# Moving the attention stage's residual loads and result stores from ScalarE's DMA queue to GpSimd's

## The chip, the cores and the metric

One core of one Trainium2 chip runs the whole model. The metric is the time of one execution on the device, in microseconds. The core has five engines that work side by side, each through its own instructions in order: TensorE (PE in the profile; PEld is its loading of weights), VectorE (DVE), ScalarE (ACT), GpSimd (POOL) and SyncE (SP), which only issues transfers. ScalarE and GpSimd can issue transfers as well; such an instruction stands in the engine's order like any other, and the profile shows it under ACTq and POOLq. Semaphores order the engines among each other.

## The reference

A batch of 32 images (3 x 96 x 96) and 32 texts (128 tokens) is turned into tokens of width 192: 36 per image, by a strided convolution and a deformable convolution, and 128 per text, by a lookup in a table that is rounded to 8 bits. The 164 tokens of a batch then go through

```python
h = jnp.concatenate([h, _L0_txt_ref(L0_txt_weight, x_txt)], axis=1)
h = h + _L0_attn_ref(_layernorm(h), Wq, bq, Wk, bk, Wv, bv, Wo, bo)   # 12 heads of 16, |i - j| <= 64
h = h + _L0_ffn_ref(_layernorm(h), w1, w2)                            # two spline layers, 192 -> 512 -> 192
```

The change touches only the second line, in two places: where `h` is read a second time, as the term on the left of the sum (the residual), and where the sum is written.

## The kernel before, in words

The stages run one after another: stem, offsets, sampling, deformable product, attention, spline layers. A stage is a block of five programs, one per engine, and all engines meet at its end. In the profiled execution the attention stage fills about 318 to 899 us of the span.

`attend_phase` (from L692) works on 16 **pairs** of batches; a batch has 164 tokens, in two groups of 82 rows. t is the pair, i = 0 or 1 the batch in it, u = t % 2 the buffer. The loops step by two pairs: pairs 0 and 1 are written out ahead, the loop covers the next ones, and the last ones are written out again (the last four on ScalarE, the last two on VectorE). Everything is pipelined over pairs by hand: in its pair t each engine also prepares pair t+1, loads and normalises t+2 and finishes t-1.

- **Loads.** `load` (L785) fetches the rows of one pair with three transfers: 36 rows per batch from `vis_scr` (L789), 46 from `txt_scr` (L790) and the other 82 from `txt_scr` (L791), all in pieces of 768 bytes. It is used twice: for `attend_x`, the input of the normalisation (13 times on ScalarE, in the second half of a pair, L1047, and three times on SyncE at the start), and for `attend_resid`, the residual (16 times on ScalarE, L1041, in the first half of pair t, for pair t).
- **Stores.** `leave` (L793) waits on `h_ready`, which VectorE raises after each of the two sums of a pair, and writes `attend_h` to `h_scr`, 328 rows of 768 bytes. ScalarE stores pair t-2 in the first half of pair t (L1040); SyncE stores the last two pairs (L827).
- **ScalarE, pair t**: first exponential (`expo`, L1030), then for i = 0 the store and the residual load, then `turned` (L1002: the high parts of the next pair's transposed x, which VectorE needs for the low parts, L894), then the second exponential and the copies out of the accumulators. For i = 1 the load of `attend_x` stands in place of store and residual load.
- **TensorE, pair t**: scores by key and by query, the transposes of the next x (L1107), the projections (first query projection L1114, which reads both parts of x), the mix of the values (L1198) and the output projection (L1210).
- **VectorE, pair t**: maxima (L871), low parts (L894, L885), `attend_oT` (L914, mixed values times reciprocal sums), the sums with the residual (`residual`, L917, its instruction at L923), reciprocals (L909), and for t+2 the normalisation (L663 to L681).
- **GpSimd**: the power -1/2 of the variance for each pair (L843), and nothing else.
- **SyncE**: the round trip `invert` (L805) for each batch: row sums out to memory and back in a wider layout (L808, L810), the reciprocals out to `rec_scr` (L813), and after their landing four broadcasts back into `attend_spread` (L817), which `attend_oT` needs.

What sets the order: each engine's program as written; VectorE's `residual` waits for the loaded residual rows and, for i = 0, until the output buffer's earlier store has landed (`h_out`). No planner is involved.

Of the kernel before, what the change touches and what calls it, by code (L numbers as in the profile page):

```python
# [39 lines left out]
PAIRS = B // 2  # L40
# [651 lines left out]
def attend_phase(nc, c, a, vis_scr, txt_scr, h_scr, w_raw, w1_in, total_scr, rec_scr):  # L692
# [16 lines left out]
    with ExitStack() as stack:  # L709
# [7 lines left out]
        resid = [sb(f"attend_resid{u}", [P, 4, D]) for u in range(2)]  # L717
# [75 lines left out]
        def leave(engine, t, u):  # L793
            engine.wait_ge(h_ready, 2 * t + 2)
            engine.dma_start(h_scr[bass.ds(t * PT, PT), :].rearrange("(n p) d -> p n d", p=ROWS),
                             h2[u][0:ROWS]).then_inc(h_out[u], 16)

        @block.sync
        def _(sp):
            for u in range(2):  # L800
                load(sp, x[u], x_in[u], u)
            sp.dma_start(wo[:], a["wo"]).then_inc(wo_in, 16)
            sp.dma_start(w_raw[:], a["w1"].rearrange("p i (h r) o -> p (i h) (r o)", h=2)).then_inc(w1_in, 16)

            def invert(t, i):  # L805

                sp.wait_ge(mix_ready, 2 * t + i + 1)
                sp.dma_start(total_scr[i], mixed[i][DH:P:32, :]).then_inc(total_out[i], 16)  # L808
                sp.wait_ge(total_out[i], 16 * t + 16)
                sp.dma_start(total[i][0:SUMS, :], total_scr[i].rearrange("j (k n) -> (j k) n", n=PART)  # L810
                             ).then_inc(total_in[i], 16)
                sp.wait_ge(inverted, 2 * t + i + 1)
                sp.dma_start(rec_scr[i].rearrange("j (k n) -> (j k) n", n=PART), rec[i][0:SUMS, :]  # L813
                             ).then_inc(rec_out[i], 16)
                sp.wait_ge(rec_out[i], 16 * t + 16)
                for j in range(4):
                    sp.dma_start(spread[i][32 * j:32 * j + 32, :],  # L817
                                 rec_scr[i, j:j + 1, :].rearrange("a n -> (a n)").partition_broadcast(32)
                                 ).then_inc(spread_in[i], 16)

            sp.wait_ge(xn_ready, 1)
            load(sp, x[0], x_in[0], 2)
            with sp.Fori(0, PAIRS) as t:
                for i in range(2):
                    invert(t, i)
            for u in range(2):
                leave(sp, PAIRS - 2 + u, u)  # L827
            for u in range(2):
                sp.wait_ge(h_out[u], 16 * (PAIRS // 2))

        @block.gpsimd
        def _(pool):
            pool.memset(minus_half[:, :], -0.5).then_inc(half_set, 1)
            pool.memset(mx[:], 0.0).then_inc(zeros_set, 1)
            for u in range(2):
                pool.memset(va[u][:, :, :, 0:DH], 0.0).then_inc(zeros_set, 1)
                pool.memset(va[u][:, :, :, DH:32], 1.0).then_inc(zeros_set, 1)
            pool.wait_ge(half_set, 1)
            pool.wait_ge(zeros_set, 5)

            def pair(t):
                pool.wait_ge(ln, LN_STEPS * t + LN_VAR)
                pool.tensor_tensor(rstd[0:ROWS, :], ve[0:ROWS, :], minus_half[0:ROWS, :], ALU.pow).then_inc(pow_done, 1)  # L843

            pair(0)
            with pool.Fori(1, PAIRS) as t:
                pair(t)

        @block.vector
        def _(dve):  # L850
# [144 lines left out]
        def _(act):  # L995
# [37 lines left out]
            def pair(tt, u, first=False, more=True, more2=True):  # L1033
                t = 2 * tt + u
                v = 1 - u
                for i in range(2):
                    expo(2 * t + i, 0)
                    if i == 0:
                        if not (isinstance(tt, int) and tt == 0):
                            leave(act, t - 2, u)  # L1040
                        load(act, resid[u], resid_in[u], t)  # L1041
                        if more:
                            for j in range(2):
                                turned(j, use(t, X[j]))
                    elif more2:
                        act.wait_ge(xn_ready, t + 2)
                        load(act, x[v], x_in[v], t + 3)  # L1047
                    expo(2 * t + i, 1)
                    if more:
                        if i == 0:  # L1050
                            for g in range(HG):
                                high(qh[:, g, :], use(t, Q[g]))
                        else:
                            values(v, 0, use(t, V[0]))
                    mix_out(2 * t + i, i, use(t, MIX[i]), first)
                    if i == 1 and more:
                        values(v, 1, use(t, V[1]))
                    if i == 0 or more:
                        high(mh[:], use(t, MAX[i]))
                    if i == 0 and more:  # L1060
                        for g in range(HG):
                            high(k1[v][:, g, :], use(t, K_[g]))
# [924 lines left out]
```

## Time and profile before

| | |
|---|---|
| three runs | 2484.45, 2494.41, 2494.56 us |
| median | 2494.41 us |
| the profiled execution | 2486.14 us |
| its span | 2484.4 us |
| busy in the span | PE 2298.2 us (93%), DVE 1897.0 (76%), ACT 1407.1 (57%), POOL 243.1 (10%) |
| granted clock of PE over the span | 0.963 of full speed |
| transfers | 116.33 MB, mean 47 GB/s |

The span runs from the first to the last instruction of the profiled execution; what its own time has beyond that is start and end. Busy shares are means over the whole program and say little about one stage. Waits and timelines name the engine that ended an idle time by "<-"; "issue" is time in which the engine waited for nothing that the profile shows as an instruction of another engine. A row of a queue (ACTq, POOLq, SPq) is the issue of a transfer, not its data.

### The profile page before, as it was taken

The numbers are of one execution on the slowest core, as the hardware profiler recorded it, in microseconds if no ns is written. First come the engines' busy times: TensorE is split into PE (matmuls) and PEld (weight loads), VectorE is DVE, ScalarE is ACT, GpSimd is POOL, SyncE is SP. The second block draws the span as 40 slices with busy tenths as digits, with TensorE's granted clock in tenths as the row PEclk, the third lists the DMA queues.
The fourth block names the chain that finished last, engine by engine and source line by source line (L and its number), as shares of the span: only waits on it lengthen the run. The fifth ranks groups of instructions, "written<-read, shape, count | busy, mean of one in ns | idle before, by whom it ended". The sixth has DMA issues, their size and how long they took to land.

```text
span 2484.4 us, 49397 instructions
## 1 busy us (share of the span) xinstructions
PE 2298.2 (93%) x20297; PEld 2148.3 (86%) x20297; DVE 1897.0 (76%) x2364; ACT 1407.1 (57%) x1391; POOL 243.1 (10%) x132
## 2 busy tenths in 40 slices
PE   7699959999999918999999999989999999999999
PEld 5366847777777718999999999989999999999999
DVE  8699745666666528766767676579999999999995
ACT  5488113444444334435344353578888888888881
POOL 6522000000000012211212121000000000000000
PEclk9799968999999958999999999999999999999999
DMA  7655131111111110000000000130000000000000
GB/s 228 167 148 152 48 142 28 44 44 41 43 43 41 37 29 17 19 15 26 19 26 19 26 18 12 45 115 23 22 25 26 23 22 22 22 22 22 22 18 10
DMA packets 99472, 116.33 MB, mean 47 GB/s; under 512 B 15287, under 2 KB 90567, under 8 KB 98631
## 3 DMA queue, kind: packets, MB, share of 16 engines
q1 hardware_dynamic: 79891, 89.95, 11.9%
q10 hardware_dynamic: 15860, 14.25, 1.9%
q0 software_dynamic: 3616, 10.54, 1.7%
q8 instruction: 89, 1.46, 0.2%
q14 instruction: 16, 0.13, 0.0%
HBM read 83.83 MB, written 30.86 MB: 46 GB/s over the span
## 4 chain that ended last, share of the span: by engine, by line
PE 62%; DVE 1%; issue 1%; DMA 0%; POOL 0%; ACT 0%; SPq 0%; POOLq 0%; DVEq 0%
PE spline_acc L1824 26%; PE spline_acc L1797 9%; PE spline_acc L1796 9%; PE spline_acc L1798 9%; PE spline_acc L1818 5%; PE spline_acc L1820 2%; PE spline_xT L1777 0%; DMA spline_x<-h_scr 0%; DVE spline_weights_low L1479 0%; DVE spline_xn L681 0%; DVE spline_f L1517 0%; DVE spline_t L1500 0%; DVE spline_b L1495 0%; DVE spline_b L1489 0%; DVE spline_a L1484 0%
## 5 line engine op out<-in xcount | busy, mean ns | idle before, releaser
L1824 PE MATMUL spline_acc<-spline_weights,spline_f 128*128 128x192 f32 x3936 | 671.9, 327 | 0.0
L1824 PEld LDWEIGHTS spline_acc<-spline_weights,spline_f 128*128 128x128 f32 x3936 | 637.1, 190 | 0.0
L1796 PE MATMUL spline_acc<-spline_f,spline_weights_high 128*128 128x328 f32 x1536 | 479.8, 312 | 7.2 <-DVE spline_f L1517 7.2
L1797 PE MATMUL spline_acc<-spline_f,spline_weights_high 128*128 128x328 f32 x1536 | 482.5, 314 | 0.0
L1798 PE MATMUL spline_acc<-spline_f,spline_weights_low 128*128 128x328 f32 x1536 | 476.3, 310 | 0.0
L1517 DVE SCALAR_TENSOR_TENSOR spline_f<-spline_n,spline_a 128x984 fp32r<-128x984 f32 x128 | 151.1, 1181 | 199.9 <-PE spline_acc L1798 198.2
L1796 PEld LDWEIGHTS spline_acc<-spline_f,spline_weights_high 128*128 128x128 f32 x1536 | 290.0, 189 | 7.4 <-issue 7.4
L1797 PEld LDWEIGHTS spline_acc<-spline_f,spline_weights_high 128*128 128x128 f32 x1536 | 289.1, 188 | 0.0
L1798 PEld LDWEIGHTS spline_acc<-spline_f,spline_weights_low 128*128 128x128 f32 x1536 | 288.8, 188 | 0.0
L1528 DVE SCALAR_TENSOR_TENSOR spline_f<-spline_n,spline_b 128x1536 f32<-128x1536 f32 x164 | 287.2, 1752 | 0.0
L1818 PE MATMUL spline_acc<-spline_weights_split,spline_f_high 128*128 128x384 f32 x656 | 218.2, 389 | 8.2 <-issue 8.2
L871 DVE TENSOR_REDUCE attend_max<-scores_by_query 82x6 f32<-82x984 f32 x128 | 150.9, 1179 | 81.7 <-PE scores_by_query L1153 81.3
L599 PE MATMUL sample_acc<-hat_weights,sample_h 120*96 120x288 f32 (+1 forms) x640 | 164.0, 414 | 21.3 <-DVE hat_weights L546 18.2
L599 PEld LDWEIGHTS sample_acc<-hat_weights,sample_h 120*96 120x96 f32 (+1 forms) x640 | 103.4, 165 | 81.6 <-issue 27.9
L1030 ACT ACTIVATE attend_probs<-scores_by_key 82x1968 f32<-82x1968 f32 x64 | 115.7, 1807 | 100.5 <-PE scores_by_key L1178 100.5
L1709 ACT ACTIVATE spline_hid<-spline_acc 128x328 f32<-128x328 f32 x64 | 28.2, 446 | 246.5 <-PE spline_acc L1798 246.5
L1820 PE MATMUL spline_acc<-spline_weights_split,spline_f_low 128*128 128x192 f32 x656 | 164.6, 251 | 0.0
L1517 DVE SCALAR_TENSOR_TENSOR spline_f<-spline_n,spline_t 128x984 fp32r<-128x984 f32 x128 | 150.5, 1176 | 0.0
L1528 DVE SCALAR_TENSOR_TENSOR spline_f_high<-spline_n,spline_v_high 128x512 fp32r<-128x512 f32 x164 | 112.6, 686 | 30.5 <-PE spline_acc L1824 29.2
L1484 DVE SCALAR_TENSOR_TENSOR spline_a<-spline_t,spline_a 128x2048 f32<-128x2048 f32 (+1 forms) x57 | 128.9, 2261 | 6.0 <-ACT spline_a L1640 6.0
L1818 PEld LDWEIGHTS spline_acc<-spline_weights_split,spline_f_high 128*128 128x128 f32 x656 | 124.0, 189 | 8.5 <-issue 8.5
L1495 DVE TENSOR_TENSOR spline_b<-spline_b,spline_a 128x2048 f32<-128x2048 f32 (+1 forms) x57 | 129.1, 2265 | 1.8
(197 smaller groups left out, 3964.7 us busy)
## 6 DMA issues: line engine op xcount, KB each, us to landing
sample_pos<-pos_scr SPq DMA_DIRECT2D x32, 540.0 KB, 4.3
hid_scr<-spline_hid SPq DMA_DIRECT2D x64, 164.0 KB, 1.8
spline_xn<-hid_scr SPq DMA_DIRECT2D x41, 256.0 KB, 3.1
attend_spread<-rec_scr SPq DMA_DIRECT2D x128, 61.5 KB, 2.2
pix_scr<-stem_by_pixel SPq DMA_DIRECT2D x32, 225.0 KB
sample_h<-pix_scr POOLq DMA_DIRECT2D x32, 225.0 KB, 4.4
spline_weights_raw<-w SPq DMA_DIRECT2D x1, 6144.0 KB, 20.4
spline_weights<-w SPq DMA_DIRECT2D x4, 1536.0 KB, 6.4
```

The lines of the kernel that those rows point to most:

```text
L599: last = nc.tensor.matmul(acc[0:C1, u, half, 0:S2], h[u][0:rows, part * C1:(part + 1) * C1], wt[0:rows, u, part, half * S2:(half + 1) * S2 ...
L871: nc.vector.tensor_reduce(mx[0:ROWS, n, 2 * h:2 * h + 2, 0:HG], sc[0:ROWS, :, 0:SC].rearrange("p j (g n) -> p j g n", n=TOK), AX_X, ALU.ma ...
L1484: nc.vector.scalar_tensor_tensor(a_[u][:, 0:cols], t_[u][:, 0:cols], 2.0, a_[u][:, 0:cols], ALU.subtract, ALU.mult).then_inc(outer_ready, 1)
L1495: nc.vector.tensor_tensor(b_[u][:, 0:cols], b_[u][:, 0:cols], a_[u][:, 0:cols], ALU.subtract).then_inc(v_ready, 1)
L1517: nc.vector.scalar_tensor_tensor(f[j % RING][:, part * HC:(part + 1) * HC], n_[u][:, cols], MAGIC + i, v[:, cols], ALU.is_equal, ALU.mult) ...
L1528: nc.vector.scalar_tensor_tensor(dst[:], n, MAGIC + i, v, ALU.is_equal, ALU.mult).then_inc(f_ready, 1)
L1796: nc.tensor.matmul(z, high, x_high, start=start, stop=False)
L1797: nc.tensor.matmul(z, high, x_low, start=False, stop=False)
L1798: last = nc.tensor.matmul(z, low, x_high, start=False, stop=stop)
L1818: nc.tensor.matmul(acc2[:, u, 0:2 * D], f_high[i][:, cols], w2_split[:, i, r].rearrange("p s o -> p (s o)"), start=start, stop=False)
L1820: last = nc.tensor.matmul(z, f_low[i][:, cols], w2_split[:, i, r, 0, :], start=False, stop=False)
L1824: last = nc.tensor.matmul(z, f_rest[i][:, cols], w2[:, i, r, :], start=False, stop=stop)
```

## The change

ScalarE no longer stores results or loads residual rows. GpSimd does both: before its loop it takes the powers of pairs 0 and 1, then for each pair t it issues the residual load of t, takes the power of t+2 and stores pair t-1; the last store follows the loop. SyncE no longer issues the last two stores and only waits for all of them. VectorE's and TensorE's programs, and ScalarE's loads of `attend_x`, are as before.

```diff
@@ SyncE
-            for u in range(2):
-                leave(sp, PAIRS - 2 + u, u)
             for u in range(2):
                 sp.wait_ge(h_out[u], 16 * (PAIRS // 2))
@@ GpSimd
-            def pair(t):
+            def power(t):
                 pool.wait_ge(ln, LN_STEPS * t + LN_VAR)
                 pool.tensor_tensor(rstd[0:ROWS, :], ve[0:ROWS, :], minus_half[0:ROWS, :], ALU.pow).then_inc(pow_done, 1)
 
-            pair(0)
-            with pool.Fori(1, PAIRS) as t:
-                pair(t)
+            def pair(tt, u, first=False, more2=True):
+                t = 2 * tt + u
+                load(pool, resid[u], resid_in[u], t)
+                if more2:
+                    power(t + 2)
+                if not first:
+                    leave(pool, t - 1, 1 - u)
+
+            power(0)
+            power(1)
+            pair(0, 0, first=True)
+            pair(0, 1)
+            with pool.Fori(1, PAIRS // 2 - 1) as tt:
+                for u in range(2):
+                    pair(tt, u)
+            for u in range(2):
+                pair(PAIRS // 2 - 1, u, more2=False)
+            leave(pool, PAIRS - 1, 1)
@@ ScalarE
                     expo(2 * t + i, 0)
                     if i == 0:
-                        if not (isinstance(tt, int) and tt == 0):
-                            leave(act, t - 2, u)
-                        load(act, resid[u], resid_in[u], t)
                         if more:
                             for j in range(2):
                                 turned(j, use(t, X[j]))
```

## Rows read from the trace of the kernel before

A timeline row gives the start in us, the length in us, engine and line, and in brackets the idle time before it and what ended it.

**Rows 1.** Busy us by stretch: length, PE, PEld, DVE, ACT, POOL; clock, DMA share, GB/s.

```profile
402.80:433.80 31.00, 29.37 (x558) 25.34 (x556) 20.54 (x44) 13.62 (x20) 1.00 (x1) 1.00 0.14 37
498.00:530.00 32.00, 29.33 (x554) 25.27 (x552) 20.77 (x43) 13.45 (x19) 1.00 (x1) 1.00 0.16 43
```

**Rows 2.** Longest wait of TensorE, 402.8 to 848.4 us: total us, times, longest us.

```profile
PE attend_spare L1114 <- DVE attend_x_rest L894: 10.2, 13, 1.0
```

**Rows 3.** ScalarE and its queue, pair 4, and the store that opens pair 5.

```profile
497.97 1.81 ACT L1030 ACTIVATE attend_probs<-scores_by_key 82x1968 f32<-82x1968 f32 x1 [1.59 <-PE scores_by_key L1178]
...
498.64 3.13 ACTq L789 DMA_DIRECT2D attend_resid<-vis_scr  x1
...
503.68 0.44 ACT L1002 ACTIVATE attend_x_high<-attend_spare 128x328 fp32r<-128x328 f32 x1 [3.91 <-issue]
...
504.67 1.80 ACT L1030 ACTIVATE attend_probs<-scores_by_key 82x1968 f32<-82x1968 f32 x1
...
516.30 0.31 ACTq L789 DMA_DIRECT2D attend_x<-vis_scr  x1
...
530.25 0.27 ACTq L795 DMA_DIRECT2D h_scr<-attend_h  x1
```

**Rows 4.** ScalarE and its queue in order of time, pair 1 (no store yet).

```profile
402.81 1.81 ACT L1030 ACTIVATE attend_probs<-scores_by_key 82x1968 f32<-82x1968 f32 x1 [1.48 <-PE scores_by_key L1178]
402.82 0.30 ACTq L789 DMA_DIRECT2D attend_resid<-vis_scr  x1
...
408.63 1.81 ACT L1030 ACTIVATE attend_probs<-scores_by_key 82x1968 f32<-82x1968 f32 x1 [0.47 <-PE scores_by_key L1178]
```

**Rows 5.** GpSimd in order of time, pair 4.

```profile
518.21 1.00 POOL L843 TENSOR_TENSOR attend_rstd<-attend_ve,attend_half 82x4 f32<-82x4 f32 x1 [31.03 <-DVE attend_ve L669]
```

**Rows 6.** VectorE in order of time, second half of pair 4.

```profile
519.18 0.54 DVE L923 TENSOR_TENSOR attend_h<-attend_spare,attend_resid 82x384 f32<-82x384 f32 x1
...
529.36 0.65 DVE L914 TENSOR_TENSOR attend_oT<-attend_mixed,attend_spread 128x492 f32<-128x492 f32 x1
```

**Rows 7.** Line 524, a load on GpSimd's queue in the sampling stage: ns min/median/max.

```profile
L524 POOL DMA_DIRECT2D sample_h<-pix_scr x32: 577/1307/1682, 85.4 to 257.4; - x32
...
DMA to landing us min/median/max: 2.9/4.4/7.8
```

**Rows 8.** SyncE's queue in order of time, pair 4.

```profile
503.37 0.30 SPq L813 DMA_DIRECT2D rec_scr<-attend_rec  x1
508.22 1.69 SPq L817 DMA_DIRECT2D attend_spread<-rec_scr  x4
...
521.90 0.31 SPq L813 DMA_DIRECT2D rec_scr<-attend_rec  x1
523.35 2.30 SPq L817 DMA_DIRECT2D attend_spread<-rec_scr  x4
```

**Rows 9.** Line 817, the broadcasts of the reciprocals.

```profile
DMA to landing us min/median/max: 1.8/2.2/3.7
```

**Rows 10.** TensorE in order of time, start of pair 5: the output projection.

```profile
530.68 0.55 PE L1210 MATMUL attend_spare<-attend_wo,attend_oT 128*82 128x192 f32 x2
```

**Rows 11.** The page's part 3: DMA queue, packets, MB, share of 16 engines.

```profile
q10 hardware_dynamic: 15860, 14.25, 1.9%
q0 software_dynamic: 3616, 10.54, 1.7%
```

**Rows 12.** VectorE, end of the attention stage.

```profile
885.13 0.67 DVE L914 TENSOR_TENSOR attend_oT<-attend_mixed,attend_spread 128x492 f32<-128x492 f32 x1 [4.88 <-DMA attend_spread<-rec_scr]
```

**Rows 13.** SyncE's queue, end of the attention stage.

```profile
890.62 0.26 SPq L795 DMA_DIRECT2D h_scr<-attend_h  x1
898.80 0.36 SPq L1366 DMA_DIRECT2D spline_identity<-identity  x1
```

**Rows 14.** DMA traffic, 890.5 to 898.5 us, 40 slices of 0.2 us: busy tenths of 16 engines, GB/s.

```profile
DMA  1100011011111111111111111111111111111000
GB/s 46 42 0 0 8 31 31 15 19 35 46 38 31 27 27 50 46 46 46 46 46 38 31 31 46 46 31 27 35 46 46 46 46 46 46 46 50 15 0 0
```

## The prediction

> **What bounds the kernel now.** I read the stretches first. Within one pair of batches the attention stage keeps TensorE busy for 29.3 us of 32.0, while VectorE has 20.8, ScalarE 13.5 and GpSimd 1.0 [rows 1]. TensorE is the bound there; work taken off another engine can give back only TensorE's gaps, 2.7 us a pair. The waits name the largest gap: the first query projection (L1114) waits for VectorE's low parts of x (L894), once in each of 13 pairs, 10.2 us in all, 1.0 at most [rows 2]. What is late behind it stands in ScalarE's order. The high parts of x (L1002) start at 503.68 after 3.91 us of idle that end on "issue", and the queue's own rows fill that gap: after a store of `h_scr` comes L789, the first of the three loads of `attend_resid`, and its issue alone takes 3.13 us [rows 3]. ScalarE works in order, so L1002 stands behind it.
>
> Pair 1 is a control that the kernel runs by itself. It issues the same three loads with no store ahead of them, and L789 takes 0.30 us; from its first exponential to its second pass 5.82 us, against 6.70 in pair 4 [rows 3, 4]. Its stretch has 1.63 us of idle TensorE, a loop pair's 2.67 [rows 1]. So the stall belongs to store and load on one queue, and 0.8 to 1.0 of its 3.9 us reach TensorE.
>
> **The change, part by part.** ScalarE loses 14 stores and 48 residual loads. It keeps its loads of `attend_x`, whose first issues in 0.31 us [rows 3]. SyncE loses the last two stores. GpSimd gains all 64 of these DMAs beside its 16 powers.
>
> *Pairs 2 to 14, a gain of 10.2 us.* With nothing to issue there, L1002 follows the transposes as in pair 1, and L1114's wait goes. By the waits that is worth 10.2 us [rows 2]; by the exponentials 6.70 - 5.82 = 0.88, times 13 = 11.4 [rows 3, 4]; by the stretches 2.67 - 1.63 = 1.04, times 13 = 13.5 [rows 1]. I take the first: it sums all 13 pairs instead of multiplying one, and the rest can be the loop's own overhead. Pairs 0 and 1 have no store ahead: nothing.
>
> *GpSimd's queue, no cost.* For pair t it now loads t's residual rows, takes the power of t+2, waits for both sums of t-1 (`h_ready`), and stores them. In pair 4 the power ends at 519.2 [rows 5] and the second sum at 519.72 [rows 6], so the store of pair 3 leaves at about 519.8, where before it left at 530.25 [rows 3], and pair 5's residual loads follow at once. This stage shows no DMA of GpSimd's. The nearest row is the sampling load, 120 rows of 1920 bytes: 1.31 us [rows 7]. By instruction four of them are 5.2 us; by rows of 768 bytes (328 in the store, 72 + 92 + 164 in the loads) 656/120 x 1.31 = 7.2 us. Either ends by 527, with the next power due 32 us after the last. The slack is 24 us; it would be gone above some 7 us a DMA. The residual rows are used two pairs on, as is the output buffer. The new wait holds back only the store and the next loads, which nobody is late for.
>
> *The neighbour, no cost within its slack.* The early store falls on SyncE's round trip for the reciprocals of batch 0 of the same pair: a write at 521.90, seen at 523.35, then four broadcasts, the last issued by 525.6 [rows 8], landed 2.2 us later [rows 9], about 527.8. `attend_oT` needs them at 529.36 [rows 6], 1.5 us on; it ends at 530.01 and TensorE takes it at 530.68 [rows 10], another 0.7. Slack: 2.2 us. Today the other round trip, batch 1's, carries the traffic: written at 503.37, seen only at 508.22, 4.85 us against 1.45 [rows 8]. Bounds for the move: nothing, or 3.4 us at the write and 3.7 - 2.2 = 1.5 at the broadcasts, 4.9 together. I take 0.5. One request on GpSimd's queue holds 10.54 MB/3616 = 2.9 KB [rows 11]; the store of the stage's end runs at up to 46 GB/s with a tenth of the 16 engines busy, about two of them [rows 14]: 23 GB/s an engine, so a turn is 0.13 us, and I allow four. The Trainium skill (DMA: Bandwidth & Descriptors, Queues, rings and completion order) has an engine change queue only at the end of a packet of up to 64 descriptors; with packets that long here the delay would be the 3.4 us of the bound, which speaks against the change.
>
> *The tail, a gain of 1.0 us.* The stage's last store leaves SyncE at 890.62 and the next stage starts at 898.80, 8.2 us later [rows 13]; its data run at 15 to 50 GB/s nearly to the end [rows 14]. From GpSimd the sampling load, 225 KB against 246, lands in 4.4 us [rows 7]; adding (328 - 120)/120 x 1.31 = 2.3 us for the further rows gives 6.7. Bounds: 4.4 (gain 3.8) and 9.2 (loss 1.0, the same transfer behind 1.31 us of issue). I take 6.7, a gain of 1.5, since the nearest row is that load. Against it, the store of pair 14 now leaves at about 879.8, ahead of the last round trip, and there `attend_oT` does wait for the broadcasts, 4.88 us [rows 12]: 0.5 lost, at most 4.9. By the skill's rule for how many engines a DMA uses (same page, Why a DMA increments its semaphore by 16 and not by 1), 82 partitions get two engines; it names an exception on GpSimd's path that spreads them over more. Under the rule the tail gains nothing and the sum is 9.7.
>
> **Sum.** 10.2 + 1.5 - 0.5 = 11.2 us. The profiled execution took 2486.14 us (span 2484.4), which gives 2474.9. It lies 8.3 below the median of the three runs, 2494.41; taken from the median, the forecast is 2483.2.
>
> **The rivals.**
>
> *The round trip becomes the wait (slower).* Place: `attend_oT` of batch 0, in each of 14 pairs. If the early store delays SyncE's write as ScalarE's does now, it is 3.4 us late, less 2.2 of slack: 1.2 a pair, 17 in all, plus 3.4 in the tail, against 11.7 gained, a loss of 9; with the broadcasts late too, 2.7 a pair, 38 + 4.9 - 11.7 = 31. That is 2503 to 2526. It decides from a delay of 3.0 us on (2.2 of slack and 0.8 of gain). For it: 4.85 against 1.45 [rows 8]. Against: the short turns worked out above. Chance 0.10.
>
> *The same, milder.* A delay of 2.5 to 2.8 us eats about half: 14 x 0.4 = 6, time 2489. Chance 0.14.
>
> *More is given back.* If the whole difference of the stretches goes, 13.5, and the last store lands in 4.4 us, the gain is 13.5 + 3.8 = 17.3: 2477. Pair 1 speaks for it; that it runs outside the loop speaks against. Chance 0.17.
>
> *GpSimd's queue becomes the limit (slower).* The Trainium skill (SBUF — State Buffer, Who interferes with whom) says that VectorE's copies in a two-port mode lock GpSimd out while it writes descriptors. Mechanism here: the power comes late from some 7.5 us a DMA on; at 10 us the four and the power take 41 us, 9 over a pair's 32, hence some 117 us in 13 pairs, 2611. No row is near: 1.68 us at most [rows 7]. Chance 0.02.
>
> *The stall stays, or moves to the loads of `attend_x`.* Then nothing changes, 2494. Those come 3.5 us before the new store, so I see little for it. Chance 0.04.
>
> **How the numbers follow.** The forecast keeps 0.53. A measurement of this kernel tells a change from none at about 0.5%, 12.5 us, and the forecast's 11.2 lies just under. A third of its chance (the 13 pairs at 11.4, a better tail) goes over: 0.18, with the larger case 0.17, less a little, 0.35 for faster. Slower: 0.10 + 0.02 = 0.12. The rest, 0.53, is no change. The range starts at 2470, the lowest run, 2484.45, less 14, since two of three runs lie 10 us above the third, and ends at 2492, above the milder rival.
>
> **What would show it.** Right: L789's issue on ScalarE's queue is gone, first to second exponential 5.8 to 5.9 us in pairs 2 to 14, L1114 no longer waits for L894, the store leaves right after the second sum, and a loop pair takes 31.0 to 31.2 us. Wrong: VectorE's L914 idle on the broadcasts inside the loop, SyncE's wait for `rec_scr` over 4 us for batch 0, GpSimd's DMAs above 3 us each, or `attend_tmp` waiting for the power.

## The result and the profile after

The changed kernel takes 2582.83 us, the median of six runs (2567.91 to 2588.44), against 2484.40 for six runs of the kernel before (2472.09 to 2494.56). Run against run the ratio is 1.0385 [1.0354 to 1.0417]: 3.9% slower, where 2483.2 and a range up to 2492 had been forecast. (The forecast's gain of 11.2 us was counted from a median of 2494.41 over three runs; six runs put that median at 2484.40.) The profiled execution took 2576.54 us.

The page of the kernel after: span, busy time by engine, granted clock in 40 slices, transfers in all and by queue.

```profile
span 2574.9 us, 49394 instructions
...
PE 2333.2 (91%) x20297; PEld 2175.0 (84%) x20297; DVE 1895.8 (74%) x2364; ACT 1408.6 (55%) x1391; POOL 326.5 (13%) x196
...
PEclk9899967978998985999999999999999999999999
...
DMA packets 102768, 116.59 MB, mean 45 GB/s; under 512 B 27287, under 2 KB 92103, under 8 KB 101927
...
q0 software_dynamic: 17696, 18.87, 3.1%
q10 hardware_dynamic: 5736, 6.69, 0.9%
```

No other engine has become the limit: the busy times are those of before but for GpSimd's issues and 35 us more on TensorE, which runs slower for part of the stage. Slices 6 to 15 of the 40 on the clock's line are this stage. The traffic is the same 116 MB, but GpSimd's queue (q0) has 14080 more packets than in [rows 11], and 12000 more packets lie under 512 bytes (15287 before).

The excess lies in the attention stage. From pair 2's first exponential to pair 15's the profiled execution of before takes 414.6 us (433.8 to 848.4) and this one 492.8 (431.0 to 923.8): 37.9 us a pair instead of 31.9, in sum 78.2. From there to the next stage it takes 66.0 us (to 989.83) instead of 50.4: 15.6 more. Pair 2 comes 2.8 us earlier. Together 91.0, the difference of the spans but for half a microsecond.

A loop pair and most of the stage, columns as in [rows 1]:

```profile
591.10:628.20 37.10, 31.53 (x557) 26.74 (x554) 20.65 (x43) 13.58 (x20) 6.14 (x5) 0.91 0.16 37
400.00:925.00 525.00, 450.43 (x7700) 382.86 (x7698) 284.71 (x584) 189.79 (x266) 84.89 (x69) 0.89 0.15 36
```

As many matmuls as in [rows 1] (557 and 554 records) keep TensorE busy 2.2 us longer, at a mean clock of 0.91, and it idles 5.6 us instead of 2.7. The waits of that stage, 400 to 960 us (total us, times, longest):

```profile
DVE attend_oT L927 <- DMA attend_spread<-rec_scr: 63.9, 14, 7.2
...
PE attend_spare L1220 <- DVE attend_oT L927: 57.0, 14, 6.7
```

TensorE's wait for the low parts of x [rows 2] is gone, and this one, 57 us in all, is there instead. Four timelines of one pair show how it comes about. GpSimd, then SyncE's queue:

```profile
579.32 1.02 POOL L841 TENSOR_TENSOR attend_rstd<-attend_ve,attend_half 82x4 f32<-82x4 f32 x1 [30.04 <-DVE attend_ve L669]
581.74 1.87 POOL L795 DMA_DIRECT2D h_scr<-attend_h  x1 [1.40 <-DVEq L940]
583.61 0.63 POOL L789 DMA_DIRECT2D attend_resid<-vis_scr  x1
584.24 1.10 POOL L790 DMA_DIRECT2D attend_resid<-txt_scr  x1
585.33 1.52 POOL L791 DMA_DIRECT2D attend_resid<-txt_scr  x1
```

```profile
583.00 0.30 SPq L813 DMA_DIRECT2D rec_scr<-attend_rec  x1
584.35 5.20 SPq L817 DMA_DIRECT2D attend_spread<-rec_scr  x4
```

VectorE and then TensorE, where the line of [rows 6] is L927 and that of [rows 10] L1220:

```profile
594.78 0.67 DVE L927 TENSOR_TENSOR attend_oT<-attend_mixed,attend_spread 128x492 f32<-128x492 f32 x1 [4.25 <-DMA attend_spread<-rec_scr]
```

```profile
595.60 4.10 PE L1220 MATMUL attend_spare<-attend_wo,attend_oT 128*82 128x192 f32 x12 [3.75 <-DVE attend_oT L927]
```

The store is issued at 581.74, the write of the reciprocals 1.3 us behind it. The write is as quick as before: seen after 1.35 us. The four broadcasts need 5.20 us to be issued, 2.30 before [rows 8], and 11.8 us pass from the write to `attend_oT`; before, the broadcasts were there some 5.9 us after it, by the median landing of [rows 9]. TensorE idles 3.75 us in one piece, and then its 12 matmuls take 4.10 us. The same twelve in the kernel before, and the granted clock of that stretch in the kernel after:

```profile
498.63 2.18 PE L1210 MATMUL attend_spare<-attend_wo,attend_oT 128*82 128x192 f32 x12
```

```profile
595.60:599.70 4.10, 4.10 (x14) 3.01 (x14) 0.94 (x1) 0.00 (x0) 0.00 (x0) 0.50 0.01 4
```

The clock of 0.50 is the lower of its two levels (1.2 GHz instead of 2.4), right behind an idle time.

The store's own transfer, and the issues of the stage (KB each, median us from issue to landing):

```profile
L795 POOL DMA_DIRECT2D h_scr<-attend_h x16: 1821/1862/1869, 421.2 to 978.5; - x16
...
DMA to landing us min/median/max: 10.7/11.6/12.4
```

```profile
attend_spread<-rec_scr SPq DMA_DIRECT2D x120, 61.5 KB, 3.0
```

It is under way for 11.6 us from its issue, over the whole of the round trip. The broadcasts' median landing, 2.2 us in [rows 9], is 3.0 for the 120 of them between 400 and 960 us, those of both batches together.

### The profile page after: what moved, and what is told of

It is laid out like the page before. It is cut to its first block, busy times and chain, and to the rows that moved or that the text cites. A ratio compares the mean times of both kernels' runs of the same rounds, so it can differ in the third digit from the quotient of the medians.

```text
span 2574.9 us, 49394 instructions
## 1 busy us (share of the span) xinstructions
PE 2333.2 (91%) x20297; PEld 2175.0 (84%) x20297; DVE 1895.8 (74%) x2364; ACT 1408.6 (55%) x1391; POOL 326.5 (13%) x196
## 2 busy tenths in 40 slices
DMA packets 102768, 116.59 MB, mean 45 GB/s; under 512 B 27287, under 2 KB 92103, under 8 KB 101927
## 3 DMA queue, kind: packets, MB, share of 16 engines
q1 hardware_dynamic: 79231, 89.45, 11.5%
## 4 chain that ended last, share of the span: by engine, by line
PE 59%; DVE 1%; issue 1%; DMA 0%; POOL 0%; ACT 0%; SPq 0%; POOLq 0%; DVEq 0%
PE spline_acc L1834 25%; PE spline_acc L1807 9%; PE spline_acc L1806 9%; PE spline_acc L1808 9%; PE spline_acc L1828 5%; PE spline_acc L1830 2%; PE spline_xT L1787 0%; DMA spline_x<-h_scr 0%; DVE spline_weights_low L1489 0%; DVE spline_xn L681 0%; DVE spline_f L1527 0%; DVE spline_t L1510 0%; DVE spline_b L1505 0%; DVE spline_b L1499 0%; DVE spline_a L1494 0%
## 5 line engine op out<-in xcount | busy, mean ns | idle before, releaser
L1220 PE MATMUL attend_spare<-attend_wo,attend_oT 128*82 128x192 f32 x384 | 101.8, 435 | 72.9 <-DVE attend_oT L927 72.9
L1220 PEld LDWEIGHTS attend_spare<-attend_wo,attend_oT 128*82 128x82 f32 x384 | 76.6, 208 | 87.2 <-issue 74.8
```

What stands on the lines that cost most here:

```text
L1220: last = nc.tensor.matmul(xb[0:ROWS, bank, n * D:(n + 1) * D], oT[i][:, g, n * ROWS:(n + 1) * ROWS], wo[:, g, :], start=(g == 0), stop=(g ...
```

## The experiments

Thirteen kernels were run. Ratios are to the kernel before, with their 95% interval. Durations "a pair" are from first exponential to first exponential: a single value is the mean of pairs 2 to 14, a range is that of pairs 2 to 13 (pair 14 is about 1 us shorter than the others in most kernels). The questions in order: is it the store or the loads; is it the queue or the moment; how much is the clock's; and what about the store does the harm.

### Store or loads

**loads_only** (against the kernel before): GpSimd loads the residual rows; the stores stay on ScalarE and SyncE.

```diff
+                load(pool, resid[u], resid_in[u], t)
+                if more2:
+                    power(t + 2)
+                if not first:
+                    pool.wait_ge(h_ready, 2 * t)
@@ ScalarE
-                        load(act, resid[u], resid_in[u], t)
```

> Only the residual loads are on GpSimd's queue, at the time of the change (after both sums of pair t-1); the stores are back where they were (ScalarE in the first half of a pair, SyncE for the last two). Theory A, collision in time: all four transfers together hit the broadcasts of batch 0, so half of the bytes costs about half: attend_oT waits 1 to 3 us a pair in place of 5, time about 2500 to 2530. Theory S, the store alone does it: no wait of attend_oT in the loop, ScalarE's queue no longer stalls, time about 2474, 10 us under the kernel before. Theory L, the loads alone do it: 2560 or more.

Measured: 2478.81 us, ratio 0.9981 [0.9961 to 1.0001]. A pair takes 31.1 to 31.3 us, and the clock is full throughout the loop. By the profile the loop is 10 us shorter than before (13 times 31.9 - 31.1); by the medians the kernel gains 4.5, and the interval does not exclude that it gains nothing.

**stores_only** (against the kernel before): GpSimd stores pair t-1, as in the change; ScalarE keeps the loads, behind a wait for the sums where its store was.

```diff
+                if not first:
+                    leave(pool, t - 1, 1 - u)
@@ ScalarE
-                            leave(act, t - 2, u)
+                            act.wait_ge(h_ready, 2 * t - 2)
                         load(act, resid[u], resid_in[u], t)
```

> Only the stores are on GpSimd's queue, at the time of the change; the residual loads are back on ScalarE, without a store ahead of them. Theory A, collision of all four: half the bytes, 2500 to 2530. Theory S, the store alone does it: 2560 or more. Theory L, the loads alone do it: no wait of attend_oT, ScalarE's load issues in 0.3 us as in pair 1 before, time about 2474.

Measured: 2565.60 us, ratio 1.0315 [1.0282 to 1.0349]. `attend_oT` waits for the broadcasts 40.0 us in 13 pairs (430 to 930 us), a pair takes 34.7 us and up to 45.3, 38.5 on average, and TensorE is at half clock for 160 us of that stretch (mean granted clock 0.84; 0.89 in the kernel after). The profiled execution, 2583.13 us, is the slowest of the four runs. ScalarE's first residual load takes 0.31 us to issue, so that the stall of [rows 3] is gone here too: it needed the store ahead of the load in ScalarE's queue.

The loads alone give a pair of the length that was forecast; the store alone costs 82 us (2565.6 - 2483.3), where the whole change costs 98 (2582.8 - 2484.4).

### Queue or moment

**gpsimd_late** (against the kernel before): all transfers on GpSimd as in the change, but in ScalarE's old place, after the first exponential of a pair, and storing pair t-2.

```diff
+                pool.wait_ge(exped, 4 * t + 1)
+                if not first:
+                    leave(pool, t - 2, u)
+                load(pool, resid[u], resid_in[u], t)
+                if more2:
+                    power(t + 2)
```

> All 64 transfers on GpSimd's queue as in the change, but issued after the first exponential of a pair (store of t-2, load of t), where ScalarE issued them before; there they meet the round trip of batch 1, which had 5 us and more of slack. Theory A, the moment of the issue is what costs: attend_oT waits for nothing in the loop, a pair takes 31.0 to 31.2 us, time about 2474 plus up to 3 for the tail. Theory Q, GpSimd's queue slows the broadcasts and the rest whenever it runs: a pair stays above 33 us, time above 2510.

Measured: 2508.91 us, ratio 1.0101 [1.0073 to 1.0129]; a pair 32.1 to 35.0 us. The store now meets the round trip of batch 1, the one that met ScalarE's store before [rows 8]. SyncE's queue, pair 4:

```profile
508.38 0.30 SPq L813 DMA_DIRECT2D rec_scr<-attend_rec  x1
516.12 1.70 SPq L817 DMA_DIRECT2D attend_spread<-rec_scr  x4
```

The write is seen after 7.7 us instead of 4.85, and here the wait of `attend_oT` is 16.3 us in 13 pairs, 2.9 at most (400 to 860 us). The moment is worth 74 us, and the version is still 26 us slower than the kernel before. Half of that lies at the stage's end: from pair 15 on `attend_oT` waits another 22.3 us, against 11.5 before. The time lies between the two theories: the lateness in the loop is small, but it is not gone.

**stores_sync** (against the kernel before): the store of pair t-1 on SyncE, right after the broadcasts of batch 0.

```diff
+            def turn(t, u):
+                invert(t, 0)
+                leave(sp, t - 1, 1 - u)
+                invert(t, 1)
```

> From the kernel before: the stores leave ScalarE for SyncE's queue, issued after batch 0's broadcasts (store of t-1); the residual loads stay on ScalarE; GpSimd issues nothing. If ScalarE's stall came from store and load on one queue, L789 issues in 0.3 us, L1114's wait of 10.2 us goes and the time is 2472 to 2476. If the store on SyncE delays batch 1's row sums or its reciprocals beyond their slack, attend_oT of batch 1 waits and the time is 2484 or more.

Measured: 2596.42 us, ratio 1.0434 [1.0390 to 1.0479], the slowest of all. SyncE's queue:

```profile
518.85 0.27 SPq L795 DMA_DIRECT2D h_scr<-attend_h  x1
520.53 1.90 SPq L808 DMA_DIRECT2D total_scr<-attend_mixed  x1
527.53 0.31 SPq L810 DMA_DIRECT2D attend_total<-total_scr  x1
```

The row sums written behind the store are seen after 7.0 us; in other positions it is 1.7 (518.20 to 519.88 in gpsimd_late). It is another wait than in the kernel after. VectorE's reciprocals (L920) wait for the sums, and the low parts of x (L905) stand behind them in VectorE's order. Waits from 440 to 930 us:

```profile
DVE attend_rec L920 <- DMA attend_total<-total_scr: 46.7, 12, 5.1
...
PE attend_spare L1125 <- DVE attend_x_rest L905: 44.8, 12, 5.0
```

So no queue is free of it: the store delays what crosses it. The 7.0 us in its own queue are not more than the 7.7 us across queues in gpsimd_late; that this version is the slowest also comes from the wait that it meets.

**scalar_moment** (against the kernel before): the moment of the change, but from ScalarE's queue: the store of pair t-1 after the last exponential of pair t.

```diff
-                            leave(act, t - 2, u)
+                            act.wait_ge(h_ready, 2 * t - 2)
@@ after the second batch's exponential
+                    if i == 1 and more and not first:
+                        leave(act, t - 1, v)
```

> From the kernel before: the store of t-1 leaves from ScalarE's queue after the last exponential of pair t, about 2 us after GpSimd issues it in the changed kernel and, as there, just when batch 0's reciprocals go round; still 82 partitions on two engines, residual loads on ScalarE as before, GpSimd issues nothing. Theory M, the moment: whichever queue carries the two-engine store, the broadcasts of batch 0 land late, attend_oT waits 2 us or more a pair, time 2500 to 2560. Theory G, GpSimd's queue makes the store slow (11.6 us to landing there): from ScalarE it lands in 7 to 8 us, attend_oT waits under 1 us a pair and the time is 2472 to 2485.

Measured: 2498.69 us, ratio 1.0050 [1.0021 to 1.0080], just below the range of theory M. `attend_oT` waits 18.5 us in 14 pairs, 2.1 at most (402 to 870 us). So about the same moment costs 15 us from ScalarE's queue and 82 from GpSimd's (stores_only); neither alone is the cause. The moments are not quite the same: here the store is issued 0.15 us before the write of the reciprocals (531.79 and 531.94), in stores_only 1.3 us before it (507.46 and 508.79), and here it is the write that is seen late, after 3.1 us (535.07), while the broadcasts are issued in 1.70.

### How much is the clock's

**filler** (against the kernel after): 16 matmuls without use ahead of the output projection's wait, for batch 0, to keep TensorE busy in it. **filler_short** has 9.

```diff
                 bank = claim(at)
+                for _ in range(9 if i == 0 else 0):
+                    nc.tensor.matmul(xb[0:ROWS, bank, 0:D], ident[:, 0:ROWS], wo[:, 0, :], start=True, stop=True)
                 pe.wait_ge(weighed, a + 1)
```

> The changed kernel with 16 more matmuls on TensorE (about 3 us at full clock) in the accumulator bank that the output projection of batch 0 is about to overwrite, before its wait for attend_oT. They compute nothing that is used. Theory C, the lost clock is half of the loss: TensorE's idle is filled, the granted clock stays at full speed in the loop (before: 102 us of half clock between 400 and 860 us of the span), a pair falls from 37.4 to 33 to 35 us and the time to 2510 to 2550. If the clock is no part of it the time stays at 2575 or rises.

Measured: 2562.22 us, ratio 1.0297 [1.0247 to 1.0347], slower than was expected; a pair takes 36.3 us. The filler took 5.43 us of TensorE and outlasted the wait by some 1.7, so it added time of its own; hence the short one.

> As filler, with 9 matmuls in place of 16. There the 16 took 5.43 us and ended about 1.7 us after attend_oT was there, so that they cost time themselves; 9 take 3.05 us and end before it. Theory C, the lost clock is half of a pair's 5.4 us: the granted clock stays at full speed in the loop and a pair takes 34.3 to 34.9 us, time 2535 to 2550. If the clock costs nothing beyond the wait, a pair stays at 36 us or more and the time at 2560 or more.

Measured: 2545.51 us, ratio 1.0223 [1.0169 to 1.0278]; TensorE in one pair, and the stage's clock:

```profile
548.68 3.15 PE L1218 MATMUL attend_spare<-attend_wo,identity_all 128*82 128x192 f32 x18
552.67 2.18 PE L1222 MATMUL attend_spare<-attend_wo,attend_oT 128*82 128x192 f32 x12 [0.84 <-DVE attend_oT L927]
```

```profile
400.00:900.00 500.00, 466.46 (x8086) 402.09 (x8082) 289.28 (x596) 193.08 (x270) 84.79 (x69) 0.99 0.16 39
```

The broadcasts are as late as ever (`attend_oT` waits 55.4 us in 13 pairs), but the clock stays at 0.99 and the projection takes 2.18 us again. With more work for TensorE the kernel is 37 us faster than the kernel after (2582.8 - 2545.5). A pair takes 34.9 us on average. Of the 6.8 us a pair between the kernel after (37.9) and the version with cut transfers below (31.1), 3.1 came back with the clock and 3.8 are the lateness itself.

### What about the store does the harm

Two theories: E, the store is long because its 82 partitions are served by few of the 16 DMA engines; R, because it consists of 328 small pieces. In either case it is its 11.6 us that cross the round trip.

**split_store** (against the kernel after): the same pieces, but 80 partitions in one transfer and 2 in another.

```diff
-            engine.dma_start(h_scr[bass.ds(t * PT, PT), :].rearrange("(n p) d -> p n d", p=ROWS),
-                             h2[u][0:ROWS]).then_inc(h_out[u], 16)
+            rows = h_scr[bass.ds(t * PT, PT), :].rearrange("(n p) d -> p n d", p=ROWS)
+            for part in (slice(0, 80), slice(80, ROWS)):
+                engine.dma_start(rows[part], h2[u][part]).then_inc(h_out[u], 16)
```

> The changed kernel with each store cut in two transfers on the same queue at the same moment: 80 partitions, then 2. Theory E, two engines: 82 partitions leave the store on about two of the 16 DMA engines for 6 us, where the broadcasts' pieces on those engines queue behind its long packets; cut so, the 80 partitions spread over all 16. Then the broadcasts land within 3 us, attend_oT waits under 1 us a pair, a pair takes 31.1 to 31.5 us and the time is 2470 to 2485. Theory R, the queue's rows or GpSimd's issue as such are the trouble: nothing gained, 2560 or more.

Measured: 2494.07 us, ratio 1.0032 [0.9999 to 1.0065]. The store in this kernel:

```profile
L797 POOL DMA_DIRECT2D h_scr<-attend_h x32: 550/619/702, 428.3 to 909.6; - x32
...
DMA to landing us min/median/max: 2.3/2.8/4.5
```

The two issues together take 1.3 us instead of 1.86, and the landing 2.8 instead of 11.6. One cut takes back 89 of the 98 us. A pair still takes 33.0 us, and `attend_oT` still waits 30.9 us in 15 pairs (400 to 960 us).

**wide_rows** (against the kernel after): 82 pieces of 3072 bytes instead of 328 of 768, 82 partitions in one transfer. The rows stand in another order in `h_scr`, so the spline stage reads other rows than the reference wants.

```diff
-            engine.dma_start(h_scr[bass.ds(t * PT, PT), :].rearrange("(n p) d -> p n d", p=ROWS),
+            engine.dma_start(h_scr[bass.ds(t * PT, PT), :].rearrange("(p n) d -> p n d", p=ROWS),
```

> The changed kernel with the store's rows in memory ordered by partition, so that a partition writes one piece of 3072 bytes in place of four of 768 (the spline stage then reads the tokens of a pair in another order; the work is the same). 82 pieces in place of 328, still 82 partitions. Theory E, two engines: the bytes per engine are the same, so the loss stays at 2550 or more, with the issue on GpSimd's queue shorter than 1.86 us. Theory R, the number of rows is what costs: most of the loss goes, under 2510.

Measured: 2489.13 us, ratio 1.0005 [0.9978 to 1.0032]; issue 0.60 us, landing 2.8 to 3.8 us. This was meant to tell E from R and did not: it is as quick as the cut one, as R wants, but its data are also spread over most engines. All transfers, 415 to 426 us in 40 slices, with its store issued at 416.1 and the store's data from 417.3 on:

```profile
DMA  1111111198662741431002414186644551111200
GB/s 47 45 47 48 39 47 47 45 293 204 201 229 90 229 137 61 26 19 3 0 0 52 88 37 99 46 113 170 184 182 155 139 155 69 54 57 43 60 0 0
```

Against it the kernel after from 581 to 594 us, with the store issued at 581.74 and its data from 584.1 on. What runs before that, at some 45 GB/s, is ScalarE's load of `attend_x`:

```profile
DMA  0113111110232321475472234224444101111311
GB/s 33 45 45 98 47 45 47 40 21 4 32 32 32 32 18 18 89 198 123 92 171 96 84 101 108 41 56 107 131 147 89 53 14 43 47 38 43 74 50 49
```

In the first the busy share goes to nine tenths and over 200 GB/s with the store's first data; in the second it is one to three tenths and 18 to 32 GB/s for two microseconds, until the residual loads join.

Split_store speaks for E and against R: all 328 pieces are still there, and what is cut is the number of partitions in one transfer. The packet records of the trace show the spread itself. The uncut store is 54 packets of 4608 bytes and 2 of 1536, two equal shares, of which 1.7 are under way at a time (stores_only, where no load shares the queue). In split_store it is 48 and 16, with up to 16 under way at once; in wide_rows 41 packets of 6144 bytes, with up to 14. The Trainium skill (DMA: Bandwidth & Descriptors, Why a DMA increments its semaphore by 16 and not by 1) has the number of engines as the largest number up to 16 that divides the outermost size, 2 for 82 and 16 for 80, with an exception for some copies from GpSimd. Both sides of it are seen here: 11.6 against 2.8 us by the rule, and wide_rows as the exception.

One thing changes along with the spread. GpSimd's queue (q0: packets, MB, share of the 16 engines) in the kernel after and then in split_store, two microseconds each from about the store's first data (584 to 586 and 497.4 to 499.4 us). In the first of them no other queue moves anything:

```profile
DMA packets 286, 0.05 MB, mean 24 GB/s; under 512 B 277, under 2 KB 277, under 8 KB 286
...
q0 software_dynamic: 286, 0.05, 22.1%
```

```profile
q0 software_dynamic: 120, 0.25, 44.0%
```

The uncut store begins with a flood of tiny packets, most of them of 24 bytes, some 400 for each store; cut, it has hardly any. Over the whole program the packets under 512 bytes are 27287 in the kernel after, 21496 in split_store, 21127 in wide_rows, 18039 in split_after and 15287 in the kernel before. So on GpSimd's queue few engines and tiny packets come and go together, and no run tells their shares apart. On ScalarE's and SyncE's queues there are none of them (15287 in scalar_moment and stores_sync), the uncut store delays its neighbours all the same, and cutting it helps (split_store_before, below): there the spread stands alone.

### Versions with cut transfers

**split_after** is the kernel after, **split_before** the kernel before, each with the store cut as above and the loads cut too; **split_store_before** is the kernel before with the store alone cut; **split_more** is split_before with the spline stage's loads of `h_scr` cut in the same way. The counts that other engines wait for are raised to match.

```diff
-            engine.dma_start(even[VIS:ROWS], txt[0:rest, b, :]).then_inc(done, 16)
-            engine.dma_start(odd[0:ROWS], txt[rest:TXT, b, :]).then_inc(done, 16)
+            engine.dma_start(even[VIS:VIS + 32], txt[0:32, b, :]).then_inc(done, 16)
+            engine.dma_start(even[VIS + 32:ROWS], txt[32:rest, b, :]).then_inc(done, 16)
+            engine.dma_start(odd[0:80], txt[rest:rest + 80, b, :]).then_inc(done, 16)
+            engine.dma_start(odd[80:ROWS], txt[rest + 80:TXT, b, :]).then_inc(done, 16)
```

> The changed kernel with stores and loads cut (80 and 2, 32 and 14), on the queues and at the moments of the change. With the stores alone cut, attend_oT still waited 30.9 us in 15 pairs. If the rest comes from the residual loads on two engines, it goes: attend_oT waits under 10 us in all, a pair takes 31.1 to 31.3 us, time 2468 to 2476. If it comes from the store at this moment, whatever its engines, a pair stays at 32 to 34 us and the time at 2485 to 2500.

> The kernel before with every store and load of the stage cut so that each transfer has a multiple of 16 partitions or a small rest (80 and 2, 32 and 14; the 36 stay), all on ScalarE's and SyncE's queues as before: two transfers per store and five per load. Theory E: the transfers leave their two engines, ScalarE's 3.13 us at L789 fall to under 0.6 us although two more are issued, L1114's wait goes, batch 1's write of the reciprocals is seen within 2 us, a pair takes 31.0 to 31.3 us and the time is 2470 to 2476. If the queue's depth in rows sets the stall, L789 still takes about 3 us and the time stays at 2484 or rises with the extra issues.

> The kernel before with only the stores cut in 80 and 2 partitions, on ScalarE's and SyncE's queues. If ScalarE's 3.1 us at L789 come from the store's 328 rows on two engines of its queue ahead of the load, they fall to under 1 us, a pair takes 31.1 to 31.4 us and the time is 2470 to 2477. If the residual loads fill the queue themselves, L789 or L791 still stalls and the time is 2480 or more.

> split_before with the first spline layer's loads of h_scr cut in 80 and 2 partitions as well. These loads are hidden behind TensorE but for the first, on whose landing the spline stage starts (7.5 us in the kernel before). Expected: that landing in 3 to 5 us, time 2464 to 2467, 3 to 4 us below split_before; if the first load is not what starts the stage, the same as split_before, 2468.

| kernel | median us | ratio to before | us a pair |
|---|---|---|---|
| split_after | 2470.27 | 0.9952 [0.9925 to 0.9979] | 31.0 to 31.3 |
| split_store_before | 2476.53 | 0.9961 [0.9938 to 0.9984] | 31.0 to 31.3 |
| split_before | 2468.36 | 0.9923 [0.9893 to 0.9954] | 31.1 to 31.3 |
| split_more | 2463.28 | 0.9891 [0.9851 to 0.9931] | 31.0 to 31.3 |

A loop pair of split_after, columns as in [rows 1]:

```profile
580.00:611.10 31.10, 29.24 (x554) 25.23 (x552) 20.66 (x43) 13.55 (x19) 5.01 (x8) 1.00 0.18 43
```

With the same queues and the same moment as the kernel after, the wait for the broadcasts is gone from the loop (two are left at the stage's end, 11.2 us), the clock is full, and a pair takes 31.1 us. It differs from split_store (2494.07 us) only in that the loads are cut as well, and is 24 us faster: beside the store, uncut loads harm too, though without it (loads_only) they do not. So the change has the pair that was forecast once the transfers are short. But the kernel before gets the same without moving anything, and then the move adds nothing (split_after 2470.27, split_before 2468.36): with the store cut, ScalarE's L789 behind it takes 0.31 to 0.62 us to issue, median 0.43, instead of 3.13 [rows 3]. The stall that the change was to remove had the same root as the harm that it did, the uncut store. The version with the lowest time, split_more, leaves all queues as they were; its interval overlaps that of split_before. Its first load of the spline stage, at 887.63, is used at 890.61, after 3.0 us:

```profile
890.61 1.14 DVE L663 BATCH_NORM_STATS2 spline_stats<-spline_x 82x6 f32<-82x192 f32 x4 [7.44 <-DMA spline_x<-h_scr]
```

In the kernel before it was 7.5 us (900.15 to 907.69).

## Why the prediction was wrong

**The gain in the loop: right in mechanism.** The wait of [rows 2] is gone, the store leaves when the second sum is there, ScalarE's stall is gone. Where nothing comes in between (loads_only, split_after), a pair takes the 31.1 us that were forecast as 31.0 to 31.2. In the time of loads_only 4.5 us of the 10.2 are seen, an amount that is not clear of noise.

**GpSimd's queue costs nothing: right for its own time.** Its four DMAs take 1.87 + 0.63 + 1.10 + 1.52 = 5.12 us a pair, against 5.2 estimated by instruction. The power is never late, and the rival on it came to nothing.

**The neighbour: this step failed.** "Bounds for the move: nothing, or 3.4 us at the write and 3.7 - 2.2 = 1.5 at the broadcasts, 4.9 together. I take 0.5." Measured it is about 5.9 us (11.8 after the write instead of 5.9), none of it at the write and all of it at the broadcasts. It is over the slack of 2.2 us: `attend_oT` waits for the broadcasts in 14 pairs, 4.6 us on average. Two readings led there. The turn of 0.13 us came from a mean of 2.9 KB for a request on q0, and that mean belongs to other transfers: with the stores and loads there, q0 gets 8.33 MB in 14080 more packets, 0.6 KB a packet. Even that mean describes none of them: most are the tiny ones, and the store's data go in packets of 4608 bytes that take 0.25 us each, twice the turn assumed, where on ScalarE's queue they go in packets of 768 bytes that take 0.04. And the only rows for such a meeting, batch 1's 4.85 us against 1.45 [rows 8], were set aside for that estimate, though they show the same store with the same neighbour. The rule of the Trainium skill on turns of whole packets (DMA: Bandwidth & Descriptors, Queues, rings and completion order), cited there, at least had the right sign. That it is packets by which the broadcasts wait was not shown: what was shown is that most of the delay goes when the store's transfer goes from 11.6 to 2.8 us, and the rest when the loads are cut too.

**The rival was the right mechanism at too low a price.** "The round trip becomes the wait" was given 2503 to 2526 and a chance of 0.10. With 5.9 us of delay its own sum would be 5.9 - 2.2 = 3.7 a pair; the idle time measured is 3.75 in the pair shown. What it lacked altogether is the second price, TensorE's clock: 37 us by filler_short, whose added matmuls are in that time. That idle time of some 4 us in this stage lowers the clock stood in no row of the kernel before's loop, where the clock is 1.00 and the gaps are 1 us.

**The tail: wrong in sign.** A gain of 1.5 us was forecast, from a store that lands in 6.7. It takes as long as the other stores from GpSimd, and the stage ends 11.4 us after it is issued, 8.2 before [rows 13]:

```profile
978.48 1.82 POOL L795 DMA_DIRECT2D h_scr<-attend_h  x1 [26.44 <-DVEq L940]
989.83 0.10 POOL L1453 MEMSET spline_half<- 128x4 f32 x1 [9.53 <-POOLq L709]
989.83 0.35 SPq L1376 DMA_DIRECT2D spline_identity<-identity  x1
```

So it is a loss of 3.2, outside the bound of 1.0 as well. The nearest row taken, the sampling load of 120 rows, has 120 partitions, and 82 are another case; the row of the same transfer from SyncE [rows 13] was nearer. A quick landing alone would not have brought the gain either: in split_after the last store lands in under 4 us, and the stage still ends 10.7 us after its issue (last section). The other 12.4 us of the 15.6 lost at the end lie before it: from pair 15's first exponential on, `attend_oT` waits for broadcasts 7.22 + 11.52 + 4.65 = 23.4 us, before 0.38 + 6.19 + 4.88 = 11.5, which is 11.9 more. The 0.5 taken against the tail was this term, and it failed with the neighbour's.

## What to carry to other kernels

Before a transfer is moved to another queue or moment, look at how long its data are under way and at what small round trip it will cross in its new place; a long transfer over few engines delayed what crossed it from each of the three queues tried. Cut such a transfer first, so that most of it has an outer size that is a multiple of 16 (here 80 + 2 of 82): cutting the store alone took away the stall that the move was for, and with the loads cut too the kernels are the fastest of this study. And an idle time of several microseconds on TensorE, repeated in a loop, has to be priced with the slower clock after it, here 3.1 us a pair beside 3.8 of the lateness itself.

## What the hardware showed that was not expected

**The end of GpSimd's last transfer does not set the stage's end.** In the kernel after, 9.53 us of idle precede GpSimd's first instruction of the next stage, which fits a landing of some 11.4 us. In split_after the store lands in 2.3 to 3.9 us, and the idle time is the same:

```profile
875.58 1.21 POOL L799 DMA_DIRECT2D h_scr<-attend_h  x2 [22.14 <-DVEq L943]
886.25 0.10 POOL L1456 MEMSET spline_half<- 128x4 f32 x1 [9.47 <-POOLq L709]
```

From SyncE's queue, in split_before, the same cut store goes out at 884.12 and the next stage starts at 887.15, 3.0 us later. From issue to next stage it is 10.7 us in the one and 3.0 in the other, some 7.6 us that come with GpSimd's queue and not with the landing; in the kernel after they would lie hidden behind it. What they are was not tried.

**An uncut transfer on GpSimd's queue is harder on its neighbours than on ScalarE's:** the store at about the same moment costs 15 us from ScalarE's queue and 82 from GpSimd's. The 12000 additional packets under 512 bytes go with the uncut transfers that GpSimd issues, 6496 with the stores (stores_only) and 5504 with the loads (loads_only), and nearly all of them go when these are cut (2752 more than before in split_after, 1664 in split_before, which issues nothing more from GpSimd). They and the larger data packets, 0.25 us each instead of 0.04, are the differences that the traces show; that either is the reason was not shown.
